# Causal attention: value products 256 columns wide for two query tiles, output work at the ends of following steps

## Chip, core and metric

The kernel runs on one core of a Trainium2 chip. The metric is the device time of one execution in microseconds (us), the median of several runs. The engines are named as in the profile: TensorE (PE; its weight loads are PEld), VectorE (DVE), ScalarE (ACT), GpSimd (POOL) and SyncE (SP).

## What is computed

A stack of six sub-layers over x of 4 batches, 1024 positions and 128 features, all in fp32, each added to a residual. The change touches only the causal attention: 16 heads of 64 features, where position i sees positions up to i.

```python
def _attention(x, ln_gamma, ln_beta, w_qkv, w_out, b_out):
    ...
    qkv = jnp.einsum('bnd,ed->bne', xn, w_qkv)
    q, k, v = jnp.split(qkv, 3, axis=-1)
    q, k, v = (reshape(q) * scale, reshape(k), reshape(v))   # 16 heads of 64
    sim = jnp.einsum('bhid,bhjd->bhij', q, k)
    sim = jnp.where(causal, mask_value, sim)
    sim = sim - jax.lax.stop_gradient(jnp.max(sim, axis=-1, keepdims=True))
    attn = jax.nn.softmax(sim, axis=-1)
    out = jnp.einsum('bhij,bhjd->bhid', attn, v)
    out = out.transpose(0, 2, 1, 3).reshape(b, n, INNER)
    return jnp.einsum('bne,de->bnd', out, w_out) + b_out
...
x = L0_attn_x                                                # 4 x 1024 x 128
x = x + 0.5 * _L0_ffn_ref(_layernorm(x), ...)
x = x + _L0_attn_ref(_layernorm(x), ...)
x = x + 0.5 * _L0_ffn_ref(_layernorm(x), ...)
x = x + 0.5 * _L1_ffn_ref(_layernorm(x), ...)                # two layers of local attention with a gated FFN
x = x + _L1_attn_ref(_layernorm(x), ...)                     # the causal attention above
x = x + 0.5 * _L1_ffn_ref(_layernorm(x), ...)
```

## The kernel before

X stays in on-chip memory (SBUF) for the whole program. The sub-layers follow one another, with a barrier between them. The causal one is `causal_attention` (L1358).

It works in 32 **units**: one batch and one pair of heads each (`UNITS = B * PAIRS`). A unit handles the 8 query tiles of 128 positions, one in each of 8 **steps** (`TICKS`, index n). The order of the query tiles is fixed by hand, so that a long one and a short one alternate. Query tile i has i + 1 key tiles to look at:

```python
TILES = (7, 0, 6, 1, 5, 2, 4, 3)
RING = 4
T_LAG, V_LAG = 2, 3
PROJECT = {1: (0, 1), 3: (2, 3), 5: (4, 5)}
```

Each tick's work is spread over the steps as a software pipeline, written out by hand in every engine's queue:

- TensorE (`unit`, L1575) issues in step n: the transposes of the first head of tick n − 2, the **scores** of tick n for both heads (L1519, two heads in the two row halves of the array, and the mask's corner at L1525), in steps 1, 3 and 5 the next unit's projections (`project`), the transposes of the second head of tick n − 2 (L1536), and then the **values** of tick n − 3 (L1549): for each key tile t and each head a product of 128 columns, the two heads in the two column halves of the array, so 2(i + 1) products, each of them two records in the profile (fp32). When the four long tiles or the four short ones are complete (each half is a bank of the accumulator `o`), `o_ready` is raised. The **output** product (L1561) of the long half follows the values of tick 7 (step 2 of the next unit), that of the short half follows the values of the next unit's tick 0 (step 3). The values of ticks 0 and 1 wait for `x_ready`, that is until the additions have read the same bank.
- VectorE (`unit`, L1633) copies the scores to `e`, negated and with the row minimum (`copy_out`, L1615), and evacuates bank 0 of the transposes to `eT` (`evacuate`, L1608). It takes the inverse of the row sums (L1620), copies `o` to `oT` (`gather`, L1625, at the starts of steps 2 and 3) and adds the output to X (`add`, L1631, at the starts of steps 3 and 4). The order in a step is: additions and gathers, evacuation of the first head, inverse of tick n − 1, copy of head 0, evacuation of the second head, copy of head 1. The scores of step n + 1 wait until both copies of step n are done.
- ScalarE (L1692) evacuates bank 1 of the transposes (L1683), takes the exponentials (L1689), and copies the projections out. Its order is evacuation, exponential of head 0, projection, evacuation, exponential of head 1, projection. Bank 1 holds the part over four key tiles of a long query tile, and the second head of a short one (`pieces`).
- GpSimd (L1731) scales `e` by the inverse (L1724), after which the transposes may start. SyncE loads the weights of the next unit.

The engines' queues run in order. Units 2 to 29 run in a hardware loop of two units; the first two and the last two are written out.

Of the kernel before, what the change touches and what calls it, by code (L numbers as in the profile page):

```python
# [1357 lines left out]
def causal_attention(nc, c, gain_d, shift_d, w_d, wo_d, bias_d):  # L1358
# [14 lines left out]
    def tile_of(n):  # L1373
        return TILES[n]

    def wide(n):
        return tile_of(n) >= 4

# [13 lines left out]
    with ExitStack() as st:  # L1392
# [14 lines left out]
        v = [sb(f"v{k}", [P, TPB, P]) for k in range(2)]  # L1407
        xv = sb("x_batch", [P, S])
        e = [[sb(f"e{r}{h}", [P, S]) for h in range(2)] for r in range(RING)]
        eT = [[sb(f"eT{r}{h}", [P, S]) for h in range(2)] for r in range(RING)]  # L1410
        nmax = sb("nmax", [P, TICKS, 2])
        total = sb("total", [P, TICKS, 2])
        inv = sb("inv", [P, TICKS, 2])
# [53 lines left out]
        with nc.Block() as block:  # L1467
# [21 lines left out]
            def _(pe):  # L1489
# [49 lines left out]

                def values(u, k, n, first):  # L1540

                    i = tile_of(n)
                    if n in (0, 1) and not first:
                        pe.wait_ge(x_ready, 2 * u - (n == 0))
                    for bank in range(2):
                        pe.wait_ge(eT_out[bank], chunks(u, n, 1 if wide(n) else bank, bank) + 1)
                    for t in range(i + 1):
                        for h in range(2):
                            m = pe.matmul(o[64 * h:64 * h + 64, i // 4, (i % 4) * P:(i % 4 + 1) * P],  # L1549
                                          v[k][:, t, 64 * h:64 * h + 64], eT[n % RING][h][:, t * P:(t + 1) * P],  # L1550
                                          start=(t == 0), stop=(t == i), skip_group_check=True)
                    if i in (4, 3):
                        m.then_inc(o_ready, 1)

                def output(u, k, half):
                    if half == 0:
                        pe.wait_ge(wo_loaded, 16 * u + 16)
                    pe.wait_ge(oT_ready, 2 * u + half + 1)
                    bank = 1 - half
                    for t in range(4):  # L1560
                        m = pe.matmul(o[:, bank, t * P:(t + 1) * P], oT[:, (4 * bank + t) * P:(4 * bank + t + 1) * P],  # L1561
                                      wo[k][:], start=True, stop=True)
                    m.then_inc(y_ready, 1)

                def trailing(u, k, n, first):

                    if n - V_LAG >= 0 or not first:
                        uv, kv, nv = earlier(u, k, n - V_LAG)
                        values(uv, kv, nv, first and n - V_LAG >= 0)
                        if nv == TICKS - 1:  # L1570
                            output(uv, kv, 0)
                        if nv == 0 and not (first and n - V_LAG >= 0):
                            output(uv - 1, 1 - kv, 1)

                def unit(u, k, first=False, last=False):  # L1575
                    for n in range(TICKS):
# [17 lines left out]
                for n in range(TICKS, TICKS + V_LAG):  # L1594
                    if n - T_LAG < TICKS:
                        transpose(u, n - T_LAG, 0, False)
                        transpose(u, n - T_LAG, 1, False)
                    values(u, k, n - V_LAG, False)
                output(u, k, 0)
                output(u, k, 1)  # L1600

# [1 line left out]
            def _(dve):  # L1603
                def evacuate(u, n, h):
                    for bank, at, tiles in pieces(n, h):
                        if bank == 0:
                            dve.wait_ge(turned[0], chunks(u, n, h, 0) + 1)
                            dve.tensor_copy(eT[n % RING][h][:, at * P:(at + tiles) * P], turn[:, 0, 0:tiles * P])\  # L1608
                               .then_inc(eT_out[0], 1)

                def copy_out(u, n, h):
# [21 lines left out]
                def unit(u, k, first=False, last=False):  # L1633
                    for n in range(TICKS):
                        turns = n - T_LAG >= 0 or not first
                        ut, kt, nt = earlier(u, k, n - T_LAG)
                        if n == 3 and not first:
                            add(u - 1, 0)
                        if n in (2, 3) and not first:
                            gather(u - 1, n - 2)  # L1640
                        if n == 4 and not first:
                            add(u - 1, 1)
                        if turns:
                            evacuate(ut, nt, 0)
                        if n > 0 or not first:
                            ui, ki, ni = earlier(u, k, n - 1)
                            inverse(ui, ni)
                        copy_out(u, n, 0)
                        if turns:
                            evacuate(ut, nt, 1)  # L1650
                        copy_out(u, n, 1)
                dve.tensor_copy(corner[:].rearrange("p a b n -> p (a b n)"), corner_f[:]).then_inc(corner_ready, 1)
                dve.wait_ge(bias_added, 1)
                over_units(dve, unit)
# [11 lines left out]
            def _(act):  # L1666
# [12 lines left out]
                def evacuate(u, n, h):  # L1679
                    for bank, at, tiles in pieces(n, h):  # L1680
                        if bank == 1:
                            act.wait_ge(turned[1], chunks(u, n, h, 1) + 1)
                            act.activation(eT[n % RING][h][:, at * P:(at + tiles) * P], turn[:, 1, 0:tiles * P],  # L1683
                                           ACT.Copy).then_inc(eT_out[1], 1)

                def exp(u, n, h):
# [228 lines left out]
```

## Time and profile before

| | |
|---|---|
| median of 3 runs | 3870.0 us (3862.85 to 3882.05) |
| the profiled execution | 3871.8 us, its span 3870.0 us |
| mean granted TensorE clock | 0.962 |
| TensorE busy | 3286.9 us, 85% of the span |
| TensorE weight loads | 2096.2 us, 54% |
| VectorE, ScalarE, GpSimd busy | 2134.3, 2102.9, 1493.1 us (55, 54, 39%) |

The page gives for each engine the time in which it was executing something. Shares are averages over stages with different limits, and the causal attention is about a third of the span (1682 to 2947 us). In the timeline, a row merges neighbouring instructions of one line: its start, the time to the end of the last of them, and their count. A matmul record's end lies behind its last column by the way through the array, so the distance from start to start is what a matmul costs, not its duration. Rows of `L1519` are the scores of the next query tile, of `L1549` the values.

### The profile page before, as it was taken

How to read it: one execution, taken by the hardware profiler on the slowest of the kernel's cores; microseconds unless marked ns; L12 is line 12 of the kernel's file. 1: busy time of each engine (PE TensorE's matmuls, PEld its weight loads, DVE VectorE, ACT ScalarE, POOL GpSimd, SP SyncE). 2: the span in 40 equal slices, each digit the busy share in tenths (PEclk: the TensorE clock that was granted, in tenths of full speed). 3: DMA queues.
4: the chain of work that ended last, by engine and by line, in shares of the span. 5: the costliest groups of instructions: out<-in, count | busy, mean ns of one | idle time of the engine just before them, and what ended most of it. 6: DMA issues, size and time to landing. Idle time of an engine off the chain costs nothing. (4 is left out here: it accounts for less than half of the span.)

```text
span 3870.0 us, 78199 instructions
## 1 busy us (share of the span) xinstructions
PE 3286.9 (85%) x29124; PEld 2096.2 (54%) x29124; DVE 2134.3 (55%) x4332; ACT 2102.9 (54%) x3388; POOL 1493.1 (39%) x1220
## 2 busy tenths in 40 slices
PE   6599998678888888669999999999995888888885
PEld 4222223445566665436666666666663556656563
DVE  4100002377777777455555555555555877777774
ACT  2499997245555555345555555555552455555552
POOL 1100000165666656223333333333332766666661
PEclk9799999899999999889999999999997999999998
DMA  1122221111111111000000000000002111111111
GB/s 32 24 38 39 36 39 21 59 32 32 28 33 32 34 30 30 12 12 9 5 6 7 6 7 6 7 5 8 5 7 66 31 33 30 31 33 29 31 30 31
DMA packets 124411, 95.80 MB, mean 25 GB/s; under 512 B 80448, under 2 KB 100544, under 8 KB 123968
## 3 DMA queue, kind: packets, MB, share of 16 engines
q1 hardware_dynamic: 122784, 89.41, 10.5%
q10 hardware_dynamic: 1440, 3.80, 0.3%
q8 instruction: 128, 2.10, 0.2%
q14 instruction: 59, 0.48, 0.0%
HBM read 22.90 MB, written 2.10 MB: 6 GB/s over the span
## 5 line engine op out<-in xcount | busy, mean ns | idle before, releaser
L1724 POOL TENSOR_SCALAR e<-e,inv 128x768 f32<-128x768 f32 (+7 forms) x512 | 375.1, 745 | 845.2 <-DVE inv L1620 845.2
L1689 ACT ACTIVATE e<-e,nmax 128x768 f32<-128x768 f32 (+7 forms) x512 | 396.2, 774 | 434.5 <-DVE e L1615 432.0
L867 POOL TENSOR_TENSOR rot<-cosine,sine 128x1024 f32<-128x1024 f32 x128 | 301.8, 2358 | 592.1 <-DVE sine L1202 592.1
L530 ACT ACTIVATE e<-slot 128x1024 f32<-128x1024 f32 x512 | 472.5, 1093 | 38.1 <-PE slot L466 38.1
L1615 DVE TENSOR_SCALAR_CACHE_REDUCE e<-slot 128x768 f32<-128x768 f32 (+7 forms) x512 | 375.6, 753 | 161.5 <-PE slot L1525 161.5
L1536 PE MATMUL slot<-ident,e 128*128 128x128 f32 x2304 | 354.7, 281 | 32.6 <-DVE eT L1608 28.3
L874 POOL TENSOR_TENSOR inv_norm<-floored,minus_half 128x16 f32<-128x16 f32 x128 | 374.1, 2922 | 10.6
L1519 PE MATMUL slot<-key,q 64*128 64x512 f32 (+3 forms) x1536 | 317.2, 518 | 38.2 <-DVE e L1615 36.9
L1608 DVE COPY eT<-slot 128x512 f32<-128x512 f32 (+3 forms) x384 | 237.7, 619 | 149.7 <-PE slot L1536 149.7
L1536 PEld LDWEIGHTS slot<-ident,e 128*128 128x128 f32 x2304 | 251.6, 141 | 113.2 <-issue 47.8
L1549 PE MATMUL slot<-eT,v 128*64 128x128 f32 x4608 | 307.9, 278 | 0.0
L921 PE MATMUL slot<-w_qk,hT 128*128 128x512 f32 x512 | 259.7, 632 | 24.1 <-DMA b<-in_local_b_dram 19.0
L481 PE MATMUL slot<-e,v 128*32 128x512 f32 x2048 | 277.4, 614 | 0.4 <-ACT e L530 0.4
L1118 ACT ACTIVATE prob<-prob 128x1024 f32<-128x1024 f32 x128 | 135.5, 1058 | 259.0 <-DVE prob L1213 259.0
L1549 PEld LDWEIGHTS slot<-eT,v 128*64 128x64 f32 x4608 | 246.3, 137 | 52.5 <-issue 52.4
L1122 ACT ACTIVATE probT<-slot 128x1024 f32<-128x1024 f32 x128 | 131.0, 1024 | 240.5 <-PE slot L965 240.5
L466 PE MATMUL slot<-query,keys 36*128 36x512 f32 x1024 | 209.3, 473 | 45.2 <-DMA keys<-n_hl 31.8
L846 POOL TENSOR_TENSOR rot<-rot,inv_norm 128x1024 f32<-128x1024 f32 x128 | 243.4, 1902 | 10.0
L1683 ACT ACTIVATE eT<-slot 128x512 f32<-128x512 f32 (+3 forms) x384 | 164.0, 427 | 152.3 <-PE slot L1536 151.9
L466 PEld LDWEIGHTS slot<-query,keys 36*128 36x128 f32 x1024 | 87.9, 187 | 268.2 <-ACT e L530 217.7
L541 DVE COPY oT<-slot 128x512 f32<-128x512 f32 x32 | 22.1, 692 | 366.0 <-PE slot L481 366.0
L937 PE MATMUL slot<-ident,rot 128*128 128x128 f32 x1024 | 146.4, 290 | 88.1 <-DVE prob L1213 81.3
(158 smaller groups left out, 6367.1 us busy)
## 6 DMA issues: line engine op xcount, KB each, us to landing
v_mix<-v SPq DMA_DIRECT2D x256, 128.0 KB, 2.3
w_qkv<-in_causal_w_dram SPq DMA_DIRECT2D x32, 192.0 KB
query<-q_hi SPq DMA_DIRECT2D x128, 32.0 KB
keys<-q_hi SPq DMA_DIRECT2D x128, 32.0 KB
query<-q_lo SPq DMA_DIRECT2D x128, 32.0 KB
keys<-q_lo SPq DMA_DIRECT2D x128, 32.0 KB
hs<-H SPq DMA_DIRECT2D x32, 128.0 KB
h1s<-H SPq DMA_DIRECT2D x32, 128.0 KB
```

The lines of the kernel that those rows point to most:

```text
L466: m = pe.matmul(out[:, h, :], keys[k][p][rows, t * P:(t + 1) * P], query[k][p][rows, half * 512:half * 512 + 512], start=True, stop=True)
L481: m = pe.matmul(c.slots[3][32 * j:32 * j + 32, half, :], v[k][:, t, j, :], e[(n - 1 + j // 2) % E_RING][:, j % 2 * 512:j % 2 * 512 + 512], ...
L530: act.activation(e[n % E_RING][:], c.slots[n % RING][:].rearrange(flat), ACT.Exp, scale=2 * SCALE).then_inc(e_ready, 1)
L867: pool.tensor_tensor(rot[:, a.j, :, :].rearrange(flat), cosine[:], sine[:], ALU.add).then_inc(rot_ready, 1)
L874: pool.tensor_tensor(inv_norm[:], floored[:], minus_half[:].broadcast_to([P, 2 * HEADS]), ALU.pow)\
L921: m = pe.matmul(bank_qk[:, half, :], hT[:, a.j * P:(a.j + 1) * P], w_qk[a.depth][:, half * 512:half * 512 + 512], start=True, stop=True)
L1519: pe.matmul(c.slots[h][:, bank, 0:hi - lo], q[k][rows, i * P:(i + 1) * P], key[k][rows, lo:hi], start=True, stop=True)
L1536: m = pe.transpose(turn[:, bank, t * P:(t + 1) * P], e[n % RING][h][:, (at + t) * P:(at + t + 1) * P], c.ident[:])
L1549: m = pe.matmul(o[64 * h:64 * h + 64, i // 4, (i % 4) * P:(i % 4 + 1) * P], v[k][:, t, 64 * h:64 * h + 64], eT[n % RING][h][:, t * P:(t + ...
L1615: dve.tensor_scalar(e[n % RING][h][:, 0:cols], c.slots[h][:].rearrange(flat)[:, 0:cols], -1.0, None, ALU.mult, ALU.min, accum_out=nmax[:, ...
L1689: act.activation(part, part, ACT.Exp, bias=nmax[:, n, h:h + 1], scale=-1.0, accum_out=total[:, n, h:h + 1]).then_inc(e_ready, 1)
L1724: pool.tensor_scalar(part, part, inv[:, n, h:h + 1], 1.0, ALU.mult, ALU.mult).then_inc(scaled, 1)
```

## The change

The values are no longer computed tick by tick. They are issued for a pair of ticks, (n − 2, n), whose query tiles are neighbours in size: (7, 6), (0, 1), (5, 4) and (2, 3). For each key tile that both see, one product of 256 columns serves both; the longer tile's last key tile follows with 128 columns. `values` is called for n = 2, 3, 6 and 7 only, that is in steps 5, 6 and (of the next unit) 1 and 2. For this, `eT` becomes one tile per head with the ring inside, and `place` orders the tiles in `o` so that a pair is adjacent. The output of the long half moves to the end of step 3, that of the short half to the end of step 4. On VectorE the gathers move to the ends of steps 2 and 3, the additions to the ends of steps 4 and 5. The values' wait for the additions moves to ticks 2 and 3. At the end of the last unit, two pairs remain in place of three single ticks. Nothing is changed outside the causal attention.

```diff
--- before.py
+++ after.py
@@ -1373,6 +1373,10 @@
     def tile_of(n):
         return TILES[n]
 
+    def place(n):
+
+        return 4 * (1 - n % 2) + n // 2
+
     def wide(n):
         return tile_of(n) >= 4
 
@@ -1407,7 +1411,7 @@
         v = [sb(f"v{k}", [P, TPB, P]) for k in range(2)]
         xv = sb("x_batch", [P, S])
         e = [[sb(f"e{r}{h}", [P, S]) for h in range(2)] for r in range(RING)]
-        eT = [[sb(f"eT{r}{h}", [P, S]) for h in range(2)] for r in range(RING)]
+        eT = [sb(f"eT{h}", [P, RING, TPB, P]) for h in range(2)]
         nmax = sb("nmax", [P, TICKS, 2])
         total = sb("total", [P, TICKS, 2])
         inv = sb("inv", [P, TICKS, 2])
@@ -1539,17 +1543,24 @@
 
                 def values(u, k, n, first):
 
-                    i = tile_of(n)
-                    if n in (0, 1) and not first:
-                        pe.wait_ge(x_ready, 2 * u - (n == 0))
+                    pair = (n - 2, n)
+                    shared = min(tile_of(m) for m in pair) + 1
+                    if n in (2, 3) and not first:
+                        pe.wait_ge(x_ready, 2 * u - (n == 2))
                     for bank in range(2):
                         pe.wait_ge(eT_out[bank], chunks(u, n, 1 if wide(n) else bank, bank) + 1)
-                    for t in range(i + 1):
+                    slot = n % RING % 2
+                    for t in range(shared):
                         for h in range(2):
-                            m = pe.matmul(o[64 * h:64 * h + 64, i // 4, (i % 4) * P:(i % 4 + 1) * P],
-                                          v[k][:, t, 64 * h:64 * h + 64], eT[n % RING][h][:, t * P:(t + 1) * P],
-                                          start=(t == 0), stop=(t == i), skip_group_check=True)
-                    if i in (4, 3):
+                            m = pe.matmul(o[64 * h:64 * h + 64, place(n - 2) // 4, place(n - 2) % 4 * P:(place(n - 2) % 4 + 2) * P],
+                                          v[k][:, t, 64 * h:64 * h + 64], eT[h][:, slot:slot + 3:2, t, :],
+                                          start=(t == 0), stop=False, skip_group_check=True)
+                    longer = max(pair, key=tile_of)
+                    for h in range(2):
+                        m = pe.matmul(o[64 * h:64 * h + 64, place(longer) // 4, place(longer) % 4 * P:(place(longer) % 4 + 1) * P],
+                                      v[k][:, shared, 64 * h:64 * h + 64], eT[h][:, longer % RING, shared, :],
+                                      start=False, stop=True, skip_group_check=True)
+                    if n in (6, 7):
                         m.then_inc(o_ready, 1)
 
                 def output(u, k, half):
@@ -1558,7 +1569,8 @@
                     pe.wait_ge(oT_ready, 2 * u + half + 1)
                     bank = 1 - half
                     for t in range(4):
-                        m = pe.matmul(o[:, bank, t * P:(t + 1) * P], oT[:, (4 * bank + t) * P:(4 * bank + t + 1) * P],
+                        at = (7 - t if bank else t) * P
+                        m = pe.matmul(o[:, bank, t * P:(t + 1) * P], oT[:, at:at + P],
                                       wo[k][:], start=True, stop=True)
                     m.then_inc(y_ready, 1)
 
@@ -1566,11 +1578,10 @@
 
                     if n - V_LAG >= 0 or not first:
                         uv, kv, nv = earlier(u, k, n - V_LAG)
-                        values(uv, kv, nv, first and n - V_LAG >= 0)
-                        if nv == TICKS - 1:
-                            output(uv, kv, 0)
-                        if nv == 0 and not (first and n - V_LAG >= 0):
-                            output(uv - 1, 1 - kv, 1)
+                        if nv in (2, 3, 6, 7):
+                            values(uv, kv, nv, first and n - V_LAG >= 0)
+                    if n in (3, 4) and not first:
+                        output(u - 1, 1 - k, n - 3)
 
                 def unit(u, k, first=False, last=False):
                     for n in range(TICKS):
@@ -1595,7 +1606,8 @@
                     if n - T_LAG < TICKS:
                         transpose(u, n - T_LAG, 0, False)
                         transpose(u, n - T_LAG, 1, False)
-                    values(u, k, n - V_LAG, False)
+                    if n - V_LAG in (6, 7):
+                        values(u, k, n - V_LAG, False)
                 output(u, k, 0)
                 output(u, k, 1)
 
@@ -1605,7 +1617,7 @@
                     for bank, at, tiles in pieces(n, h):
                         if bank == 0:
                             dve.wait_ge(turned[0], chunks(u, n, h, 0) + 1)
-                            dve.tensor_copy(eT[n % RING][h][:, at * P:(at + tiles) * P], turn[:, 0, 0:tiles * P])\
+                            dve.tensor_copy(eT[h][:, n % RING, at:at + tiles, :].rearrange("p t q -> p (t q)"), turn[:, 0, 0:tiles * P])\
                                .then_inc(eT_out[0], 1)
 
                 def copy_out(u, n, h):
@@ -1634,12 +1646,6 @@
                     for n in range(TICKS):
                         turns = n - T_LAG >= 0 or not first
                         ut, kt, nt = earlier(u, k, n - T_LAG)
-                        if n == 3 and not first:
-                            add(u - 1, 0)
-                        if n in (2, 3) and not first:
-                            gather(u - 1, n - 2)
-                        if n == 4 and not first:
-                            add(u - 1, 1)
                         if turns:
                             evacuate(ut, nt, 0)
                         if n > 0 or not first:
@@ -1649,6 +1655,10 @@
                         if turns:
                             evacuate(ut, nt, 1)
                         copy_out(u, n, 1)
+                        if n in (2, 3) and not first:
+                            gather(u - 1, n - 2)
+                        if n in (4, 5) and not first:
+                            add(u - 1, n - 4)
                 dve.tensor_copy(corner[:].rearrange("p a b n -> p (a b n)"), corner_f[:]).then_inc(corner_ready, 1)
                 dve.wait_ge(bias_added, 1)
                 over_units(dve, unit)
@@ -1680,7 +1690,7 @@
                     for bank, at, tiles in pieces(n, h):
                         if bank == 1:
                             act.wait_ge(turned[1], chunks(u, n, h, 1) + 1)
-                            act.activation(eT[n % RING][h][:, at * P:(at + tiles) * P], turn[:, 1, 0:tiles * P],
+                            act.activation(eT[h][:, n % RING, at:at + tiles, :].rearrange("p t q -> p (t q)"), turn[:, 1, 0:tiles * P],
                                            ACT.Copy).then_inc(eT_out[1], 1)
 
                 def exp(u, n, h):
```

## Rows read from the trace of the kernel before

Unit 2041.32 to 2080.57 stands for all: steps begin with the rows of group 3.

**Rows 1.** The windows: busy us (and instructions) of each engine, granted clock, DMA.
```profile
1727.20:2904.90 1177.70, 1116.61 (x10081) 776.51 (x10080) 643.69 (x1680) 626.84 (x1501) 380.21 (x510) 1.00 0.02 7
```

**Rows 2.** Waits of TensorE, 1727.2 to 2904.9 us: total us, times, longest.
```profile
PE slot L1519 <- DVE e L1615: 32.6, 88, 0.5
PE slot L1536 <- DVE eT L1608: 24.6, 62, 0.5
```

**Rows 3.** Timeline, TensorE, scores: start, length, line, operands, count, idle before.
```profile
2041.32 1.99 PE L1519 MATMUL slot<-key,q 64*128 64x512 f32 x8
...
2046.47 0.49 PE L1519 MATMUL slot<-key,q 64*128 64x128 f32 x4 [0.48 <-DVE e L1615]
...
2051.62 1.77 PE L1519 MATMUL slot<-key,q 64*128 64x512 f32 x8
...
2056.69 0.70 PE L1519 MATMUL slot<-key,q 64*128 64x256 f32 x4
...
2063.21 1.56 PE L1519 MATMUL slot<-key,q 64*128 64x512 f32 x8
...
2067.41 0.92 PE L1519 MATMUL slot<-key,q 64*128 64x384 f32 x4 [0.43 <-DVE e L1615]
...
2073.05 1.35 PE L1519 MATMUL slot<-key,q 64*128 64x512 f32 x8
...
2076.77 1.13 PE L1519 MATMUL slot<-key,q 64*128 64x512 f32 x4 [0.19 <-DVE e L1615]
...
2080.57 1.99 PE L1519 MATMUL slot<-key,q 64*128 64x512 f32 x8
```

**Rows 4.** The same timeline: value bursts, transposes, corner, output.
```profile
2044.04 0.88 PE L1549 MATMUL slot<-eT,v 128*64 128x128 f32 x12
2045.34 0.66 PE L1536 MATMUL slot<-ident,e 128*128 128x128 f32 x4 [0.42 <-DVE eT L1608]
...
2057.22 0.28 PE L1525 MATMUL slot<-corner 64*128 64x128 bf16 x4
...
2059.46 1.97 PE L1549 MATMUL slot<-eT,v 128*64 128x128 f32 x32
2061.35 1.16 PE L1561 MATMUL slot<-w_out,oT 128*128 128x128 f32 x8
2062.35 0.93 PE L1536 MATMUL slot<-ident,e 128*128 128x128 f32 x7
```

**Rows 5.** Timeline of VectorE in the same unit.
```profile
2043.44 1.23 DVE L1615 TENSOR_SCALAR_CACHE_REDUCE e<-slot 128x1024 f32<-128x1024 f32 x1 [1.37 <-PE slot L1525]
...
2044.59 0.69 DVE L1608 COPY eT<-slot 128x512 f32<-128x512 f32 x1
2045.20 1.21 DVE L1615 TENSOR_SCALAR_CACHE_REDUCE e<-slot 128x1024 f32<-128x1024 f32 x1
...
2062.66 0.69 DVE L1631 TENSOR_TENSOR X<-slot,X 128x512 f32 x1 [3.55 <-PE slot L1561]
```

**Rows 6.** Timeline of ScalarE, step 7 of the same unit.
```profile
2078.77 0.72 ACT L1689 ACTIVATE e<-e,nmax 128x512 f32<-128x512 f32 x1 [1.10 <-DVE e L1615]
...
2079.49 0.47 ACT L1683 ACTIVATE eT<-slot 128x384 f32<-128x384 f32 x1
```

**Rows 7.** Windows in the local stage and here, and a page group.
```profile
902.20:905.60 3.40, 1.67 (x37) 1.29 (x36) 3.37 (x4) 1.65 (x3) 3.32 (x3) 1.00 0.09 22
905.70:909.00 3.30, 3.30 (x14) 2.78 (x13) 2.31 (x4) 2.39 (x4) 3.22 (x2) 0.50 0.08 18
909.10:912.50 3.40, 3.40 (x45) 2.25 (x44) 1.18 (x3) 1.02 (x1) 0.44 (x1) 1.00 0.35 79
3704.50:3707.90 3.40, 1.39 (x33) 1.01 (x32) 3.37 (x4) 0.97 (x3) 3.18 (x3) 1.00 0.02 4
2043.30:2046.70 3.40, 2.50 (x30) 1.81 (x27) 3.26 (x6) 1.65 (x4) 0.34 (x1) 1.00 0.00 0
...
L1118 ACT ACTIVATE prob<-prob 128x1024 f32<-128x1024 f32 x128 | 135.5, 1058 | 259.0 <-DVE prob L1213 259.0
```

## The prediction

> **What bounds the kernel now.** I read the views in this order: the page's busy rows, the windows of the causal stage, TensorE's waits there, then the timeline of one loop unit on each engine. TensorE is the busiest engine of the page. The causal stage runs from about 1682 to 2947 us; its 30 loop-shaped units fill 1727.2 to 2904.9, so one unit (one head pair of one batch) takes 1177.7 / 30 = 39.26 us, with TensorE busy 1116.6 of 1177.7 us and a granted clock of 1.00 throughout [rows 1]. TensorE's only waits there are for VectorE: 32.6 us at the scores and 24.6 us at the transposes, 57.2 / 30 = 1.9 us a unit [rows 2]. So TensorE bounds the stage, except in a few steps, and the question is which.
>
> **The measure** I use is the start of the scores of each of the eight steps, S0 to S7 [rows 3]: 2041.32, 2046.47, 2051.62, 2056.69, 2063.21, 2067.41, 2073.05, 2076.77, and the next S0 at 2080.57. The intervals are 5.15, 5.15, 5.07, 6.52, 4.20, 5.64, 3.72 and 3.80 us. Rows with idle time before the scores are S1, S5 and S7: there VectorE was late; the other intervals are TensorE's own work.
>
> **Prices.** The burst of 32 records at L1549 lasts 1.97 us, of which .27 is the last record's own tail: sixteen pairs (one record for each head, side by side in the two column halves) at .109 us, plus .05 to start [rows 4]. From the last transpose to the first record of a burst, and from its last record to what follows, it is .20 us each (the burst of 32 starts at 2059.46, its last pair at 2061.15, the output at 2061.35 [rows 4]), where seven transposes in .93 − .27 = .66 us follow each other at .66 / 6 = .11 [rows 4]. A burst over k key tiles so costs .05 + (2k − 1) × .109 + .30, the .30 being two handovers less the .11 that would stand there anyway: 1.99, 1.77, 1.55, 1.34, 1.11, .90, .68 and .46 us for k = 8 to 1, together 9.80.
> A pair 256 columns wide is not in a value burst of this trace. The nearest row is the scores of the 256-wide tile: 2056.69 to the corner at 2057.22 is .53 us for two pairs and a .10 start, .215 a pair [rows 3, 4]. I take .216. The low end is no less than twice .109 less one start gap, .213; the high end, the two column halves no longer side by side, is .43. The 128-wide pairs run side by side, and nothing in the edit takes that away, so I stay at the low side.
> A shared burst of m key tiles costs .05 + 2m × .216 + .109 + .30: 3.48 us for tiles (7,6), m = 7; 2.62 for (5,4), m = 5; 1.76 for (2,3), m = 3; .89 for (0,1), m = 1; together 8.75. The columns streamed are the same, 36 × 128 for each head; 72 weight loads become 40, but they were hidden. What is saved is four pairs of handovers less a bit: 9.80 − 8.75 = **1.05 us of TensorE work a unit**. The output of four tiles with its handover costs 1.00 us (2061.35 to 2062.35) wherever it stands [rows 4].
>
> **Step by step.** What counts is where the work goes. The pairs are issued in steps 1, 2, 5 and 6; steps 0, 3, 4 and 7 lose their bursts; the outputs move from steps 2 and 3 to 3 and 4.
> - S0 to S1, 5.15 us, unchanged. VectorE's chain sets it: the first copy starts at 2043.44, then 1.23, evacuation .69 and second copy from 2045.20, 1.21 long, to 2046.41 [rows 5]; S1 starts at 2046.47. The transposes before S1 wait for the evacuation too, 2045.34 [rows 4]. The burst removed here (k = 3, .68) stood wholly under that chain: it gives nothing and TensorE idles .68 more.
> - S1 to S2: 5.15 − 1.34 (k = 5) + 2.62 = 6.43.
> - S2 to S3: 5.07 − 1.11 − 1.00 (output) + 1.76 = 4.72. VectorE's chain of this step, two copies of 896 columns and an evacuation, is about as long (an estimate from [rows 5], the copies scaled to 896: 1.9 us of scores, then 2.7).
> - S3 to S4: 6.52 − 1.99 = 4.53; one output stays. The transposes-to-output handover is taken as .11; if it is .20 it costs .1.
> - S4 to S5: 4.20, VectorE's chain; TensorE's own work is about 3.8 with the second output in it.
> - S5 to S6: 5.64 − 1.77 + 3.48 = 7.35.
> - S6 to S7: 3.72, VectorE's chain; TensorE's own work is 3.5.
> - S7 to S0: TensorE's work falls to 3.80 − 1.55 = 2.25, but a new wait shows. Tile 4's transposes need the second bank, which ScalarE must first empty of tile 2. ScalarE's exponential starts 2.00 us after S7 and takes .72, its evacuation starts at 2079.49 and lasts .47 [rows 6]: 3.19 after S7, plus .05 to wake TensorE, plus .20 to the scores: 3.45.
>
> Sum: 5.15 + 6.43 + 4.72 + 4.53 + 4.20 + 7.35 + 3.72 + 3.45 = **39.55 us** against 39.26: .29 us a unit more, 8.7 us for 30 units. The work saved comes back as waiting, because the bursts were taken from steps in which they covered another engine's chain and put where TensorE is the last anyway.
> In the last unit the two remaining pairs stand behind the last transposes: 2.62 + 1.76 where 1.34 + 1.11 stood, 1.9 more, less about .5 that the transposes come earlier: +1.5 (bounds 0 to 3). The first unit comes out even by the same rows.
>
> **The moved VectorE work.** VectorE now sits 3.55 us in the queue before an addition [rows 5], waiting for the output; that and its like vanish, since gathers and additions come a step or two after their data. Nobody gains: the work queued behind (evacuation, inverse, copies) was in time for TensorE. In the new place each .69 us stands in front of the next evacuation, whose reader, the second half of the transposes, comes over 1.4 us later; uncovered it would cost .69. The added wait of the pair bursts on both additions has 2 to 3 us of cover; behind it are queued the next transposes. SyncE's load of the output weights waits for a later output, with a unit to spare. GpSimd's order is unchanged.
>
> **The clock.** This turns the sum. Around S1 TensorE will run two thin stretches with the burst between them gone. In 2043.30 to 2046.70 it is busy 2.50 of 3.40 us today; less the burst's .88 us [rows 4] that is 1.62. In the local stages a stretch with 1.67 of 3.40 us busy, at 1.00, was followed by one at a granted clock of 0.50 (1.2 GHz), then back to 1.00 [rows 7]. Ten such places follow stretches of 1.39 to 1.67 us busy in the trace (the two ends stand in [rows 7]), among 128 rounds of the loop [rows 7]; most rounds have a thin stretch and no fall, so it comes down to how they lie. Each fall here would land on S1 to S2, pure TensorE work: 3.4 us at half speed, nearly all streaming, loses 1.6 us, with nothing later to absorb it. Between none and every unit (0 to 48 us) I take 18 of 30, since the thin stretch is longer here than there: 18 × 1.6 = **29 us**.
> The Trainium skill ("TensorE: Matmul & The Clock Gate", Part 1: The HAM clock gate) says that the throttled state is the default and that PE activity releases it; by that rule a rearrangement that leaves TensorE idler for a while can pay twice. [rows 7] agree with it.
>
> **Rivals.**
> 1. Forecast: the table above and the falls. 3871.8 (the profiled execution) + 8.7 + 1.5 + 29 = 3911; that execution lies 1.8 above the median of the three runs, so 3909. Own range 3892 to 3928. Chance .55.
> 2. No falls: TensorE keeps 1.00 as in all of [rows 1], whose thinnest stretch is far busier than the new one. 3870 + 10.2 = 3880, range 3870 to 3889. This is the case on the other side, "not slower": the clock decides it. Chance .29.
> 3. The handovers pay in full: the stage is TensorE's, 30 × 1.05 = 31.5 us comes out, 3838. For it speaks that TensorE is busy 95% here; against it, the chain before S1 and the ScalarE wait, which don't depend on TensorE. It decides at S7 to S0 and S0 to S1: they would have to shrink by .68 and 1.2. Chance .08.
> The Trainium skill ("TensorEngine Tiling (Array Packing)", Key Properties) says that changing tiling mode drains the TensorE; read as a price for every change, eight fewer a unit argue for this rival. The .20 against .11 of [rows 4] is that price, but only where nothing else is last.
> 4. The wide pairs don't run side by side: 32 × .215 = 6.9 us a unit, 3870 + 10 + 206 = 4086. Chance .03. The remaining .05 is for something I don't see, either way.
>
> **Range and chances.** From 3868 to 3930 it holds nearly all of rivals 1 and 2, 8 in 10 with the unseen allowed for. A measurement of this kernel can tell about 0.5%, 19 us, from no change: below 3851 faster, above 3889 slower. Faster .10, same .31, slower .59.
>
> **What would show it.** Right: 80 value records a unit in four bursts, 64 of them 256 wide; S0 to S1 still 5.15; S5 to S6 at 7.35; a wait of the transposes before S0 for ScalarE's eT at L1683's successor; longer waits for VectorE before S1; a mean clock below 1.00 in the stage, with S1 to S2 at 6.4 in some units and 8.0 in others. Wrong: S7 to S0 near 2.3, or a pair pitch away from .216. If the clock stays 1.00 and units take 39.5, it is the second case.

## The result

| | before | changed |
|---|---|---|
| median | 3870.7 us (3862.9 to 3882.1) | 3924.1 us (3919.2 to 3934.8) |
| profiled execution | 3871.8 | 3924.1 |
| mean granted clock | 0.962 | 0.950 |

The ratio is 1.0141, with a 95% interval of 1.01 to 1.0181. One execution of the changed kernel took 10202.8 us at a mean clock of 0.41; with it the median is 3929.4, and it is left out of the table and of the ratio.

The page of the changed kernel: span and instructions, then busy time of each engine.

```profile
span 3922.2 us, 73849 instructions
PE 3296.5 (84%) x26950; PEld 2037.7 (52%) x27076; DVE 2138.0 (55%) x4332; ACT 2108.2 (54%) x3388; POOL 1495.0 (38%) x1220
```

Two thousand matmul records fewer, and TensorE is busy 10 us longer. The windows say why: the 30 loop-shaped units (answering to [rows 1]), then two stretches around one S1 (columns as there).

```profile
1732.70:2958.00 1225.30, 1129.58 (x8161) 724.11 (x8160) 648.66 (x1681) 630.33 (x1501) 381.83 (x510) 0.97 0.02 6
2061.40:2064.80 3.40, 1.69 (x14) 1.19 (x16) 3.39 (x6) 1.79 (x4) 0.04 (x1) 0.99 0.00 0
2064.90:2068.20 3.30, 3.30 (x10) 1.45 (x7) 0.72 (x6) 1.86 (x5) 2.14 (x2) 0.51 0.00 0
```

The units take 1225.3 us where they took 1177.7, and the granted clock is 0.97 where it was 1.00. The second row is the stretch before S1: TensorE is busy 1.69 us of 3.40 there, where it had been 2.50 [rows 7]. In the third row, right behind it, the clock is 0.50 but for the edge. The timeline of TensorE from S7 of one unit to S2 of the next:

```profile
2055.77 1.13 PE L1523 MATMUL slot<-key,q 64*128 64x512 f32 x4 [0.17 <-DVE e L1627]
...
2058.01 0.65 PE L1540 MATMUL slot<-ident,e 128*128 128x128 f32 x4 [0.52 <-POOL e L1734]
2059.02 0.33 PE L1540 MATMUL slot<-ident,e 128*128 128x128 f32 x1 [0.36 <-ACT eT L1693]
2059.28 1.99 PE L1523 MATMUL slot<-key,q 64*128 64x512 f32 x8
...
2061.31 0.77 PE L1540 MATMUL slot<-ident,e 128*128 128x128 f32 x5
2063.30 0.66 PE L1540 MATMUL slot<-ident,e 128*128 128x128 f32 x4 [1.22 <-DVE eT L1620]
2064.44 0.56 PE L1523 MATMUL slot<-key,q 64*128 64x128 f32 x4 [0.48 <-DVE e L1627]
...
2065.15 3.45 PE L1502 MATMUL slot<-x_batch,w_qkv 128*128 128x512 f32 x4
...
2072.52 1.77 PE L1523 MATMUL slot<-key,q 64*128 64x512 f32 x8
```

S7 to S0 is 2059.28 − 2055.77 = 3.51 us, with a wait for GpSimd and, behind it, for ScalarE. S0 to S1 is 5.16 as before, with 1.22 us of waiting for VectorE's evacuation where it was .42 [rows 4]. The projection in step 1 is the reader's sign for the clock: four records in 3.45 us; in a unit without a fall (S1 at 1737.88) the same row reads 1.98. S1 to S2 is 8.08.

TensorE's waits over the 30 units (answering to [rows 2]):

```profile
PE slot L1540 <- DVE eT L1620: 37.0, 30, 1.3
PE slot L1523 <- DVE e L1627: 32.1, 88, 0.5
PE slot L1540 <- POOL e L1734: 15.4, 30, 0.5
PE slot L1540 <- ACT eT L1693: 11.5, 31, 0.4
```

The sum is 96 us where it was 57: two waits are new, GpSimd's and ScalarE's, about once in each unit.

Reading the starts of the scores in all units gives this table (us, medians over the 30 loop-shaped units; a "fall" is a stretch at a granted clock of 0.50, "short" is a unit without one). S1 to S2 stands for units without a fall; a fall adds 1.65 to it and to nothing else.

| | S0–S1 | S1–S2 | S2–S3 | S3–S4 | S4–S5 | S5–S6 | S6–S7 | S7–S0 | short unit | falls in 30 |
|---|---|---|---|---|---|---|---|---|---|---|
| before | 5.16 | 5.15 | 5.06 | 6.52 | 4.20 | 5.64 | 3.72 | 3.81 | 39.26 | 0 |
| forecast | 5.15 | 6.43 | 4.72 | 4.53 | 4.20 | 7.35 | 3.72 | 3.45 | 39.55 | 18 |
| changed | 5.16 | 6.43 | 4.77 | 4.42 | 4.20 | 7.35 | 3.72 | 3.51 | 39.57 | 23 |

So the profiled difference of 52.2 us divides, to the rounding, as 30 × .31 = 9.3 us for the steps, 23 × 1.65 = 38.0 for the clock in the loop-shaped units, and 4.4 for the last unit and the tail (from its S0 to the end of the stage's last output product). The stages ahead of this one were 5.5 us longer and those behind it 5.2 us shorter in that execution. They are the same code, and the start of the first scores lay anywhere between 1687.6 and 1699.5 us in the traces of this study.

### The profile page after: what moved, and what is told of

The parts are those of the page before. It is cut to its first block and busy times, and to the rows that moved or that the text cites. A ratio compares the mean times of both kernels' runs of the same rounds, so it can differ in the third digit from the quotient of the medians.

```text
span 3922.2 us, 73849 instructions
## 1 busy us (share of the span) xinstructions
PE 3296.5 (84%) x26950; PEld 2037.7 (52%) x27076; DVE 2138.0 (55%) x4332; ACT 2108.2 (54%) x3388; POOL 1495.0 (38%) x1220
## 5 line engine op out<-in xcount | busy, mean ns | idle before, releaser
L1540 PE MATMUL slot<-ident,e 128*128 128x128 f32 x2304 | 366.8, 284 | 71.0 <-DVE eT L1620 42.0
L1555 PE MATMUL slot<-eT,v 128*64 128x256 f32 x2048 | 250.8, 387 | 0.0
L1099 ACT ACTIVATE sq<-slot 128x1024 f32<-128x1024 f32 x128 | 131.3, 1025 | 155.8 <-PE slot L921 155.5
```

Source lines behind the costliest of these rows:

```text
L1540: m = pe.transpose(turn[:, bank, t * P:(t + 1) * P], e[n % RING][h][:, (at + t) * P:(at + t + 1) * P], c.ident[:])
L1555: m = pe.matmul(o[64 * h:64 * h + 64, place(n - 2) // 4, place(n - 2) % 4 * P:(place(n - 2) % 4 + 2) * P], v[k][:, t, 64 * h:64 * h + 64], ...
```

## The experiments

The theory was that two things act: bursts taken from steps where they stood under another engine's chain, and a fall of the clock that the thin stretch before S1 brings on. The rivals were the wide products themselves and the moved output and VectorE work.

### Filling the thin stretch

```diff
-                        for t in range(tiles):
+                        for t in (*range(tiles), *(range(tiles) if (n, h) == (6, 1) else ())):
                             m = pe.transpose(turn[:, bank, t * P:(t + 1) * P], ...
```

> The changed kernel with the five second-head transposes of step 0 each issued twice (the second writes the same values again), so that TensorE has 0.55 us more to do in the thin stretch ahead of S1, under VectorE's chain. Theory (TensorE's idling there brings the clock down): S0 to S1 stays 5.16 us, no fall to 0.50 in the loop units instead of 23, every unit 39.57 us, so 23 x 1.65 = 38 us less than the changed kernel: 3924 - 38 = 3886 us. Rival (the falls are not brought by that idling, but by the wide products or by chance): the falls stay, the time stays at 3924 us or a little more for the added work.

Measured: 3887.6 us (3880.0 to 3893.6), 1.0033 of before (1.0019 to 1.0047). The units, and one passage from S0 to the projection:

```profile
1729.50:2916.50 1187.00, 1107.74 (x8313) 726.16 (x8312) 648.65 (x1680) 627.32 (x1501) 381.83 (x510) 1.00 0.02 7
```

```profile
2046.02 1.99 PE L1523 MATMUL slot<-key,q 64*128 64x512 f32 x8
...
2048.05 1.31 PE L1540 MATMUL slot<-ident,e 128*128 128x128 f32 x10
2050.04 0.65 PE L1540 MATMUL slot<-ident,e 128*128 128x128 f32 x4 [0.68 <-DVE eT L1620]
2051.18 0.49 PE L1523 MATMUL slot<-key,q 64*128 64x128 f32 x4 [0.48 <-DVE e L1627]
...
2051.71 1.98 PE L1502 MATMUL slot<-x_batch,w_qkv 128*128 128x512 f32 x4
```

Ten transposes for five, the wait behind them shorter by what they take, S1 still 5.16 after S0, and the projection at 1.98. All 30 units take 39.57 us (1187.0 / 30) and the clock stays at 1.00 in them. Giving TensorE useless work took 38.3 us out of the 30 units (1225.3 to 1187.0) and 36 us out of the median. The falls come from the idling there, and they are the larger part of the loss.

### Narrow products in the same places

```diff
-                    slot = n % RING % 2
-                    for t in range(shared):
...
+                    for one in pair:
+                        for t in range(tile_of(one) + 1):
+                            for h in range(2):
+                                m = pe.matmul(o[64 * h:64 * h + 64, place(one) // 4, place(one) % 4 * P:(place(one) % 4 + 1) * P],
+                                              v[k][:, t, 64 * h:64 * h + 64], eT[h][:, one % RING, t, :],
+                                              start=(t == 0), stop=(t == tile_of(one)), skip_group_check=True)
```

> The changed kernel with its four bursts where they are, but of products 128 columns wide, one query tile after the other (72 products a unit instead of 40). Theory (the change's effect is where the bursts stand, not their width): 36 x 2 pairs at 0.109 us against 32 at 0.216 and 8 at 0.109, 7.85 against 7.78 us a unit, 2 us in all; the falls stay at about 23; 3926 us. Rival (the wide products cost more than two narrow ones, or bring the clock down): S5 to S6 clearly under 7.35 us and the time nearer to 3870 to 3890 us. Rival (the width saves something that other costs hide): clearly over 3935 us.

Measured: 3923.9 us (3919.9 to 3928.9), 1.0128 (1.011 to 1.0147), the changed kernel's time. The largest burst (tiles 7 and 6), first here, then in the changed kernel:

```profile
2040.97 3.50 PE L1555 MATMUL slot<-eT,v 128*64 128x128 f32 x60
```

```profile
2089.07 3.24 PE L1555 MATMUL slot<-eT,v 128*64 128x256 f32 x28
2092.14 0.39 PE L1560 MATMUL slot<-eT,v 128*64 128x128 f32 x4
```

Sixty narrow records take 3.50 us; twenty-eight wide and four narrow run from 2089.07 to 2092.53, 3.46. A short unit takes 39.64 us against 39.57, and 23 of 30 units have a fall. The width in the change's title is worth .07 us a unit; what the change does to the time does not come from the width.

### Output work back in its old place

```diff
-                    if n in (3, 4) and not first:
-                        output(u - 1, 1 - k, n - 3)
+                    if n in (2, 3) and not first:
+                        output(u - 1, 1 - k, n - 2)
...
+                        if n == 3 and not first:
+                            add(u - 1, 0)
+                        if n in (2, 3) and not first:
+                            gather(u - 1, n - 2)
+                        if n == 4 and not first:
+                            add(u - 1, 1)
                         if turns:
                             evacuate(ut, nt, 0)
...
-                        if n in (2, 3) and not first:
-                            gather(u - 1, n - 2)
-                        if n in (4, 5) and not first:
-                            add(u - 1, n - 4)
```

> The changed kernel with outputs, gathers and additions back at their places of the kernel before (outputs in steps 2 and 3, gathers at the starts of steps 2 and 3, additions at the starts of 3 and 4). Theory: S2 to S3 is TensorE's own work and gets one output of 1.00 us more, 4.77 to 5.8; S3 to S4 keeps one output; S4 to S5 loses one but stays at VectorE's 4.20; so 1.0 us a unit more, 31 us in all, with the falls as they are: 3924 + 31 = 3955 us. Rival (the moved VectorE and output work is what made the change slower): the time falls towards 3870 to 3900 us.

Measured: 3929.5 us (3928.6 to 3938.0), 1.0146 (1.0128 to 1.0163); 3955 was expected. The mechanism held: S2 to S3 is 5.70 (+.93), S4 to S5 stays 4.20, a short unit takes 40.55 us, +.98. What missed is the count: 8 falls, not 23. So the move of the outputs is a good part of the change, worth about 30 us by the steps, and the clock had taken nearly all of it back. Without it the moved bursts alone make a unit 1.29 us longer than before (40.55 for 39.26), not .31.

### A longer unit with the outputs moved

```diff
-                        for t in range(tiles):
+                        for t in (*range(tiles), *(range(tiles) if (n, h) == (0, 1) else ())):
                             m = pe.transpose(turn[:, bank, t * P:(t + 1) * P], ...
```

> The changed kernel with the eight second-head transposes of step 2 each issued twice (the second writes the same values again): 0.9 us more of TensorE work in every unit, in a step that is TensorE's own, far from the thin stretch. It brings the unit without a fall to the length that e3_old_output has, 40.5 us. Theory (the thin stretch is the same in every unit, and the unit's length sets in how many of them it lies so that the clock falls): 8 or so falls as there and not 23, so 28 us added and 24 taken off: 3928 us, S2 to S3 at 5.7. Rival (the output's old place is what spared e3_old_output the falls): still 23 falls, 3952 us.

Measured: 3933.0 us (3926.2 to 3938.6), 1.0147 (1.0121 to 1.0174). A short unit takes 40.44 us, S2 to S3 5.64, and 10 of 30 units have a fall. The rival's 23 falls and 3952 us are out: with the outputs where the change puts them, the longer unit alone brings the count down. Behind the first few units, the changed kernel has a fall in five units, then one without, and again; this one has one in every third, the last experiment one in every fourth.

### The thin stretch alone, in the kernel before

```diff
-                        values(uv, kv, nv, first and n - V_LAG >= 0)
+                        if nv == 6:
+                            values(uv, kv, 5, False)
+                        if nv != 5:
+                            values(uv, kv, nv, first and n - V_LAG >= 0)
```

> The kernel before with one move alone: the burst of tile 2 (3 key tiles, 128 columns wide) goes from step 0 to step 1, ahead of that step's own burst. Theory: S0 to S1 stays 5.16 us with 0.68 us more waiting, S1 to S2 grows by 0.38, a unit without a fall 39.64 us, 12 us in all; and the clock, which never fell in this stage before, falls in 8 to 25 units: 3895 to 3925 us. Rival (the falls need the wide products or the moved output work): no fall, 3884 us.

Measured: 3929.4 us (3927.1 to 3932.6), 1.0136 (1.0113 to 1.0159). One burst of six pairs, moved by one step in the kernel before, costs what the whole change does. The timeline from S0 into step 1:

```profile
2056.17 1.99 PE L1519 MATMUL slot<-key,q 64*128 64x512 f32 x8
...
2060.19 0.66 PE L1536 MATMUL slot<-ident,e 128*128 128x128 f32 x4 [1.23 <-DVE eT L1614]
2061.33 0.49 PE L1519 MATMUL slot<-key,q 64*128 64x128 f32 x4 [0.48 <-DVE e L1621]
...
2061.86 3.41 PE L1498 MATMUL slot<-x_batch,w_qkv 128*128 128x512 f32 x4
...
2065.91 1.97 PE L1549 MATMUL slot<-eT,v 128*64 128x128 f32 x32
```

The same 1.23 and .48 us of waiting as in the changed kernel, then the projection at half speed; 18 of 30 units have it. So neither wide products nor moved output work are needed for the falls. I was wrong on a smaller point: S1 to S2 grew by .65, not .38. The burst joins another in step 1, so no handover is added there, but none is saved where it counted either: the one that it leaves was under VectorE's chain.

The same kernel with the transposes of step 0 doubled, as in the first experiment:

> The kernel of e8_before_thin with the five second-head transposes of step 0 issued twice, as in e1_fill. Theory: no fall is left and every unit takes 39.91 us, as the units without a fall in e8_before_thin: 0.65 x 30 = 20 us over the kernel before, 3892 us. Rival (the moved burst does something beside the thin stretch): 3905 us or more.

Measured: 3896.7 us (3887.1 to 3900.0), 1.0058 (1.0037 to 1.008). All 30 units take 39.92 us:

```profile
1726.60:2924.00 1197.40, 1128.54 (x10231) 793.52 (x10230) 643.66 (x1680) 626.77 (x1502) 380.22 (x510) 1.00 0.02 7
```

1197.4 / 30 = 39.91, and the clock is 1.00. The moved burst did nothing else in these units than add its .65 us and bring on the falls.

### ScalarE's order in step 7

```diff
+                        if n == 7:
+                            evacuate(ut, nt, 1)
                         exp(u, n, 0)
...
-                        if turns:
+                        if turns and n != 7:
                             evacuate(ut, nt, 1)
```

> The changed kernel with ScalarE's evacuation of the second bank in step 7 put ahead of the exponential of head 0. Theory (ScalarE is what S7 to S0 waits for): the last transpose before S0 no longer waits; then GpSimd's scaling is next, and S7 to S0 falls from 3.51 to about 2.9 us; a unit without a fall 38.95 us, some 19 us less before the falls are counted, whose number may change with the unit's length (0 to 30 of 1.65 us): 3870 to 3915 us, and 38.95 in the shortest units decides. Rival (another engine holds S0): S7 to S0 stays at 3.5 us.

Measured: 3902.4 us (3896.4 to 3903.0), 1.0064 (1.004 to 1.0087). TensorE's waits over the 30 units, and the transposes before S0:

```profile
PE slot L1540 <- DVE eT L1620: 37.0, 30, 1.3
PE slot L1523 <- DVE e L1627: 32.1, 88, 0.5
PE slot L1540 <- POOL e L1736: 15.3, 30, 0.5
```

```profile
2048.70 0.76 PE L1540 MATMUL slot<-ident,e 128*128 128x128 f32 x5 [0.51 <-POOL e L1736]
```

The wait for ScalarE is gone, the five transposes run on in one row, and GpSimd is what they wait for. S7 to S0 is 2.92, a short unit 38.99 us, .27 under the kernel before; 16 falls (of 1.69 us here) put the time above it all the same.

### Spreading the largest pair over the waits

The two mechanisms together say where the bursts should go. eT gets eight places instead of four, so that a pair can wait, and the pair of tiles 7 and 6 leaves step 5:

```diff
-        eT = [sb(f"eT{h}", [P, RING, TPB, P]) for h in range(2)]
+        eT = [sb(f"eT{h}", [P, TICKS, TPB, P]) for h in range(2)]
...
-                    slot = n % RING % 2
-                    for t in range(shared):
+                    slot = n - 2
+                    for t in (range(shared) if part is None else (range(CUT), range(CUT, shared))[part]):
...
-                        if nv in (2, 3, 6, 7):
+                        if nv in (3, 6, 7):
                             values(uv, kv, nv, first and n - V_LAG >= 0)
+                        if nv == 4:
+                            values(u, k, 2, first, part=0)
+                        if nv == 5:
+                            values(u - 1, 1 - k, 2, False, part=1)
```

> The changed kernel with eight places instead of four in eT, so that the pair of tiles 7 and 6 can be computed later: its first two key tiles in step 7, the other five and the last 128 columns in step 0 of the next unit, where VectorE's chain stands. Theory: S5 to S6 falls by 3.48 to about 3.9 us, S7 to S0 stays near 3.5, S0 to S1 grows from 5.16 to about 5.85 (2.62 us of burst in 1.94 us of waiting), the rest stays: about 36.8 us a unit, no falls, 30 x 2.45 us less than the kernel before: 3797 us, range 3780 to 3815. Rival (TensorE's work alone sets the stage, so that moving a burst gains nothing): one handover more than the changed kernel, which could gain only the falls: 3890 us.

Measured: 3828.1 us (3824.2 to 3832.4), 0.9882 (0.9863 to 0.9902). No falls, S0 to S1 at 5.84 and S7 to S0 at 3.51 as expected, a unit of 37.75 us; but S5 to S6 is 4.86 and not 3.9. TensorE's waits and the row of S6:

```profile
PE slot L1524 <- ACT v L1695: 21.4, 30, 0.7
PE slot L1524 <- DVE e L1636: 17.7, 58, 0.4
```

```profile
2060.10 1.35 PE L1524 MATMUL slot<-key,q 64*128 64x512 f32 x8 [0.72 <-ACT v L1695]
```

The transposes' waits are gone, and a wait that I had not priced ends last: the scores of step 6 need the bank that ScalarE's copy of the last projection empties. It leaves room for a part of the burst in step 5 (edit against the version before):

```diff
-    CUT = 2
+    CUT = (1, 3)
...
+                        if nv == 2:
+                            values(u, k, 2, first, part=0)
                         if nv == 4:
-                            values(u, k, 2, first, part=0)
+                            values(u, k, 2, first, part=1)
                         if nv == 5:
-                            values(u - 1, 1 - k, 2, False, part=1)
+                            values(u - 1, 1 - k, 2, False, part=2)
```

> The kernel of e4_spread with the pair of tiles 7 and 6 in three parts: one key tile in step 5, where S6 waits 0.98 us for ScalarE's copy of the last projection, two in step 7, four and the last 128 columns in step 0. Theory: S5 to S6 stays at 4.86 us, S0 to S1 falls by two pairs, 5.84 to 5.41: 37.3 us a unit, 13 us less than e4_spread, 3815 us. Rival (the extra handover costs more than it hides): S5 to S6 grows, 3828 us or more.

Measured: 3819.2 us (3816.8 to 3822.3), 0.9851 (0.9829 to 0.9874): S5 to S6 stays 4.86, S0 to S1 is 5.41, a unit 37.32 us. The two waits now, and the units:

```profile
PE slot L1524 <- DVE e L1638: 17.6, 58, 0.4
PE slot L1524 <- ACT v L1697: 7.1, 30, 0.2
```

```profile
1732.80:2852.70 1119.90, 1094.85 (x8163) 707.22 (x8162) 648.65 (x1681) 624.85 (x1501) 381.82 (x510) 1.00 0.02 7
```

TensorE is busy in 98% of them, waits 25 us where it waited 57 [rows 2], and this version is 1.5% faster than the kernel before.

The same with narrow products only, in the same parts:

> The kernel of e6_three_parts with products 128 columns wide only, the same parts in the same steps. Theory (where the products stand is all that counts): 72 pairs at 0.109 us for 40, 0.05 to 0.1 us a unit more, 37.4 us, no falls: 3821 us. Rival (with the waits filled, the wide products begin to pay, since a hidden weight load is no longer hidden): 3835 us or more.

Measured: 3819.2 us (3807.9 to 3825.2), 0.9846 (0.982 to 0.9872), a unit of 37.38 us. Even with TensorE busy in 98% of the units' time, as here too, the wide products are worth .06 us a unit, too little to see in the time.

## Why the prediction came out as it did

The direction, the mechanism and the range held: 3909 us was forecast, 3924 measured, in the forecast's own range of 3892 to 3928. That the time lies in the range is in part luck: the number of falls was a guess, and at 1.6 us each the range holds every count from 8 to 30. Taken by its steps:

**The step table** was right to .02 us a unit (39.55 for 39.57). No interval is off by more than .11. S3 to S4 came out .11 shorter, because an output behind transposes starts .11 us after the last of them and takes .90 us to the next row (2079.96 to 2080.86), where one behind a burst takes 1.00. S7 to S0 is .06 and S2 to S3 .05 longer. One price in it was misread: the burst taken from step 0 has three key tiles, which by the list of prices cost .90 us, not .68. The wait that it had covered grew by .80 (.42 to 1.22). The sum is not touched, since VectorE's chain sets S0 to S1 either way.

**S7 to S0** named ScalarE, and undoing that wait confirmed it (3.51 to 2.92). It left out GpSimd, for which the transposes just ahead of it wait .52 us, and which remains.

**The price of a fall** was forecast at 1.6 and is 1.65 us. **Their number** is the term that was mis-sized: 18 forecast, 23 measured, 8.3 us; with the price, 38.0 for 28.8, the clock's term was 9.2 us short. There was no row to take it from, and the experiments show why a row could hardly have given it: the same thin stretch gives 8, 10, 16, 18 or 23 falls in 30 units, by how long a unit is (only the doubled transposes of step 2 changed that length alone, in the experiment "A longer unit with the outputs moved").

**The last unit and the tail** cost 4.4 us, not 1.5 (bounds 0 to 3): of it .9 is in the last unit's steps, which have no projections and so other last waits than the loop's; the tail behind it took 3.5. The forecast had no fall of the clock there, and there is one: from 2996.6 us on the clock is 0.50 for 3.4 us, and the burst of tiles 5 and 4 runs into it. The burst in the tail, its last part behind it, and then the same burst in a unit:

```profile
2997.02 3.82 PE L1555 MATMUL slot<-eT,v 128*64 128x256 f32 x20
3000.67 0.39 PE L1560 MATMUL slot<-eT,v 128*64 128x128 f32 x4
```

```profile
2068.97 2.38 PE L1555 MATMUL slot<-eT,v 128*64 128x256 f32 x20
2071.18 0.39 PE L1560 MATMUL slot<-eT,v 128*64 128x128 f32 x4
```

From start to start that is 3.65 us for 2.21, so 1.4 of the tail's 3.5 us is the clock. Half of the miss on this term is so a fall too.

Together 9.2 + 2.9 + .6 for the unit's .02 make 12.7 of the 13 us between the 3911 forecast for the profiled execution and its 3924.

**The rivals.** That the clock stays at 1.00 was false, but its time was right for the kernel that has no falls: 3880 forecast, 3887.6 measured with the filled stretch, which has all else of the change; that is 10 us forecast and 12.5 measured over the median of the kernel before that was taken beside it (3875.1). That the handovers pay in full failed at the two places named: S0 to S1 did not shrink at all, and S7 to S0 by .30 us of the burst's 1.55. The .20 us between rows of different tiling is there in the changed kernel too (2092.26, the last pair of the largest burst, to 2092.46, the transposes), and it has eight fewer in a unit, but six of them stood in steps 0, 4 and 7, where VectorE or ScalarE was last. The Trainium skill ("TensorEngine Tiling (Array Packing)", Key Properties) says that changing the tiling mode drains the TensorE. The .20 us agree with it; what a drain costs the time, though, went here by which engine was last in its step. That wide pairs don't run side by side is out: 14 pairs in 3.07 us, .216 each after .05 to start.

**The moved output work** was put down as worth nothing to anyone behind VectorE's waits. No run moves VectorE's part alone. The experiment that undoes both moves makes a unit .98 us longer, and the output product's own 1.00 us leaves nothing of that for VectorE. But the output product's second new place, S4 to S5, has a wait of VectorE's to cover it, which is where the .98 us a unit come from: with the outputs back, TensorE waits 59.3 us for `eT` of VectorE and not 37.0, once more in each unit, in step 4. The table had this, the text did not say it.

**The price of S5 to S6** in the spread version failed by 1.0 us, for the usual reason: when 3.5 us of work are taken from a step, the next thing that TensorE depends on has to be looked for, here the projection's copy. In the kernel before it lay under TensorE's work and showed in no row of TensorE's waits.

## What to carry to other kernels

Write down, step by step, which engine is last, and price a moved burst by the step that it leaves and the step that it joins: with the outputs at their new place in both, the same products gave +1.4% or −1.5% by their place alone, and their width gave nothing. Where a move leaves a busy TensorE with a thin stretch, look at the granted clock behind it; a few useless transposes there are cheaper than the fall, and real work there is cheaper still. An experiment that lengthens a loop can change the number of falls, so compare units without a fall with each other and count the falls apart.

## What the hardware showed

Doubling five transposes, .55 us of work in a unit of 39.6, removed all 23 falls in the loop-shaped units; transposes alone were enough for that. A fall lowers the granted clock from 1.00 to 0.50 for 3.4 us and costs 1.65 us where TensorE is last (1.63 to 1.69 in the six kernels that have falls in these units). It always starts near the same place of a unit, between .1 us before S1 and 1.2 us behind it.

With the same thin stretch, the number of falls follows the unit's length in a regular beat: five units of six at 39.57 us, mostly four of five at 39.64, three of five at 39.91, three of six at 38.99, one of three at 40.44, one of four at 40.55.

The starts of the falls in the trace's record of the clock show what the beat looks like. In the changed kernel two neighbouring falls start 40.96 us apart, or twice that, and a unit with a fall takes 41.22 us. So each fall starts about .3 us earlier in its unit than the one before, from 1.2 us behind S1 down to 0, and then one unit goes without. Where one unit in three has a fall the starts are 122.88 us apart, where one in four has it 163.84 us; with three in six they are 40.96 us apart within a group and 157.01 from group to group. Which units have a fall so goes by how the unit's length lies against distances that do not stretch with it. What sets these distances was not tried.
